# A fused attention and FFN layer on one core: the head of the program reordered, row norms on ScalarE, and new tables of the order

## The reference

```python
xn = _layernorm(x, axis=-1)                          # (x - m) / sqrt(v + eps)
# attention: 16 heads of 8 channels, scale 1/sqrt(8), causal
Q = _rope(split_heads(xn @ wq.T), 10000.0)
K = _rope(split_heads(xn @ wk.T), 10000.0)
V = split_heads(xn @ wv.T)
scores = jnp.einsum('bhqd,bhkd->bhqk', Q, K) * scale
scores = jnp.where(causal_mask, -jnp.inf, scores)
out = jnp.einsum('bhqk,bhkd->bhqd', jax.nn.softmax(scores), V)
attn = merge_heads(out) @ wo.T
ffn = jnp.einsum('bsk,nk->bsn', xn, CB) * (SCB * (1.0 / 127.0)) + bias
return x + attn + ffn
```

## Time and profile before

| | us |
|---|---|
| median of 3 runs | 260.01 |
| lowest and highest | 258.69 and 260.51 |
| the profiled execution | 259.88 |
| its span | 258.2 |
| TensorE busy | 240.1 (93%) |
| VectorE busy | 218.7 (85%) |
| ScalarE busy | 183.6 (71%) |
| GpSimd busy | 103.6 (40%) |

### The profile page before, as it was taken

The page is one execution under the profiler, slowest core; times in us unless marked ns, Lnnn a source line. Parts: engine busy times, 40 slices in busy tenths (PEclk is TensorE's granted clock), DMA queues, the critical chain, the costliest instruction groups (busy, mean ns, idle before and its releaser), DMA issues.

```text
span 258.2 us, 10150 instructions
## 1 busy us (share of the span) xinstructions
PE 240.1 (93%) x4294; PEld 124.1 (48%) x4294; DVE 218.7 (85%) x594; ACT 183.6 (71%) x360; POOL 103.6 (40%) x169
## 2 busy tenths in 40 slices
PE   6888896888999999999999999999999999999945
PEld 6546541233344555554554465445555554436334
DVE  7899268999999999989999998999889989962072
ACT  2045732273997888779788878889889799999701
POOL 7570724749856391293233032304401430440300
PEclk9999998699999999999999999999999999999997
DMA  7625758620230467162027103700770210010602
GB/s 196 220 66 150 202 120 156 144 46 4 67 85 23 106 165 129 44 165 67 5 81 165 29 4 103 158 18 3 192 163 5 90 41 4 3 44 20 182 10 84
DMA packets 23559, 22.96 MB, mean 89 GB/s; under 512 B 2757, under 2 KB 20549, under 8 KB 23513
## 3 DMA queue, kind: packets, MB, share of 16 engines
q1 hardware_dynamic: 23368, 22.05, 34.3%
q10 hardware_dynamic: 144, 0.26, 0.4%
HBM read 13.70 MB, written 8.39 MB: 86 GB/s over the span
## 4 chain that ended last, share of the span: by engine, by line
PE 72%; DVE 13%; ACT 5%; DMA 4%; SPq 2%; issue 2%; POOL 1%; ACTq 0%
PE psA L918 22%; PE psB L918 20%; PE psV L990 18%; DVE prod L802 8%; ACT ring L697 3%; PE psB L906 2%; PE psB L901 2%; PE psA L1030 2%; DMA qs<-shiftsT 2%; SPq L384 2%; DMA rest<-o_scratch 2%; PE psA L872 1%; DVE rest L815 1%; PE psB L872 1%; ACT xnT L639 1%
## 5 line engine op out<-in xcount | busy, mean ns | idle before, releaser
L802 DVE CUSTOM_DVE_ANT_0 prod<-psA,cmask 128x128 f32<-128x128 f32 (+7 forms) x256 | 177.9, 754 | 16.7 <-PE psA L918 15.6
L697 ACT ACTIVATE ring<-psB 128x512 f32<-128x512 f32 x288 | 154.5, 608 | 33.6 <-PE psB L918 30.7
L918 PE MATMUL psB<-qs,ks 128*32 128x512 bf16 (+3 forms) x1536 | 99.2, 327 | 0.5 <-DMA qs<-shiftsT 0.2
L918 PE MATMUL psA<-ks,qs 128*32 128x512 bf16 (+3 forms) x1536 | 94.7, 334 | 5.3 <-DVE mx L802 4.5
L990 PE MATMUL psV<-ring,va 128*32 128x512 f32 (+3 forms) x768 | 76.0, 486 | 0.1
L918 PEld LDWEIGHTS psB<-qs,ks 128*32 128x32 bf16 x1536 | 40.8, 96 | 48.6 <-ACT ring L697 24.2
L559 POOL TENSOR_SCALAR_AFFINE_SELECT ring<-ring 128x512 f32<-128x512 f32 x64 | 40.0, 642 | 48.2 <-ACT ring L697 48.2
L918 PEld LDWEIGHTS psA<-ks,qs 128*32 128x32 bf16 x1536 | 34.2, 96 | 43.8 <-DVE mx L802 28.0
L539 POOL CAST shifts<-mx 128x16 bf16<-128x16 f32 x16 | 3.2, 198 | 71.0 <-DVE mx L802 71.0
L990 PEld LDWEIGHTS psV<-ring,va 128*32 128x32 f32 x768 | 22.5, 110 | 16.6 <-issue 8.9
L802 DVE DVE_READ_ACCUMULATOR2_ANT mx<- 128x1 f32 x256 | 21.3, 83 | 0.0
(11 more groups left out here) (89 smaller groups left out, 157.0 us busy)
## 6 DMA issues: line engine op xcount, KB each, us to landing
qs<-q_scratch SPq DMA_DIRECT2D x48, 96.0 KB
ks<-k_scratch SPq DMA_DIRECT2D x48, 96.0 KB
o_scratch<-ot SPq DMA_DIRECT2D x12, 256.0 KB, 2.6
q_scratch<-ot SPq DMA_DIRECT2D x20, 128.0 KB, 2.5
k_scratch<-ot SPq DMA_DIRECT2D x12, 128.0 KB, 2.5
x_sb<-x SPq DMA_DIRECT2D x4, 256.0 KB, 4.5
rope_sb<-rope SPq DMA_DIRECT2D x2, 512.0 KB, 6.8
rot<-o_scratch SPq DMA_DIRECT2D x3, 256.0 KB, 3.5
```

The costliest lines, as they stand in the source:

```text
L697: act.activation(ring[:, s % P_RING, k * HALF:(k + 1) * HALF], bank_b(e % B_RING), ACT.Exp)\
L802: last = dve.tensor_tensor_reduce(masked_scores[:, u % 2, at:at + w], psA[:, (u % 2) * SEQ + at:(u % 2) * SEQ + at + w], cmask[:, SEQ - w: ...
L918: mm = pe.matmul(psum[strip:strip + STRIP, at:at + size], keys[:, strip:strip + STRIP], queries, start=True, stop=True)
```

## The change

1. The third part of chunk 3 moves from GpSimd to VectorE, and the one of chunk 1 on VectorE stands ahead of rows 2 and 3's norms, which VectorE no longer does. ScalarE normalises rows 2 and 3: Identity with scale rstd and bias mean_shift = -mean x rstd, two new small steps of GpSimd per row (scales, mean_shifts). Row 3's statistics stand on VectorE behind chunk 3's third part.
2. Four tasks, not five, stand ahead of the first unit. The transposes of row 3 and their wait for four saved tasks stand behind unit 0 (TURN_AFTER), task v1 and the others behind later units.
3. ScalarE's queue stores the third part of chunk 1 and loads the three key stacks of quad 0's first half; SyncE no longer does. SyncE stores quad 0's shifts ahead of the loads of quads 1 and 2.
4. Chunk 5 is kept in ot, not in xn, so the save of quad 1's half 0 waits for its third part.
5. All tables are new.

```diff
-TASKS = [("v", 0), ("ffn", 0), ("late", 4), ("late", 5), ("v", 1), ("ffn", 1), ("late", 6), ("late", 7),
-         ("max", 0)]
-FIRST_TASKS = 5
+TASKS = [("v", 0), ("ffn", 0), ("late", 4), ("late", 5), ("v", 1), ("ffn", 1), ("max", 0), ("late", 6), ("late", 7)]
+FIRST_TASKS = 4
-TASK_AFTER = {(5, 0): 0, (5, 1): 1, (6, 0): 2, (6, 1): 2, (7, 0): 3, (7, 1): 3, (8, 0): 8}
+TURN_AFTER = 0
+TASK_AFTER = {(4, 0): 2, (4, 1): 4, (5, 0): 5, (5, 1): 7, (6, 0): 10, (7, 0): 11, (7, 1): 13, (8, 0): 15, (8, 1): 18}
...
 VALUE_BANK = [
-    [7, 8, 13, 27, 29, 31, 33, 39, 44, 45],
+    [7, 9, 13, 28, 30, 32, 35, 40, 45, 50],
...
-    [11, 20, 22, 26, 29, 32, 35, 37, 37, 38],
+    [12, 15, 17, 21, 24, 27, 30, 35, 35, 36],
...
 SAVE_BANK = [
...
-    [23, 43],
+    [18, 40],
...
-LATE_SPLIT = [[-2, -2, 11], [-2, 10, 23], [8, 17, 35], [11, 22, 45]]
+LATE_SPLIT = [[-2, 9, 15], [-2, 19, 25], [-2, 21, 25], [19, 40, 59]]
-LATE_BANK = [[1, 4], [7, 28], [26, 30], [28, 49]]
+LATE_BANK = [[7, 9], [8, 30], [29, 31], [33, 52]]
...
-PROJECT_BANK = [269, 276, 296]
-TURN_FIRST = 292
+PROJECT_BANK = [261, 271, 290]
+TURN_FIRST = 285
...
+            def mean_shifts(g):
+                bt = slice(4 * g, 4 * g + 4)
+                pool.wait_ge(rstd_ready, g + 1)
+                pool.tensor_tensor(mean_shift[:, bt], mv[:, bt, 0], rstd[:, bt], ALU.mult).then_inc(shift_step, 1)
+                pool.wait_ge(shift_step, g - 1)
+                pool.tensor_scalar(mean_shift[:, bt], mean_shift[:, bt], -1.0, None, ALU.mult).then_inc(shift_ready, 1)
...
+            def normalise(g):
+                act.wait_ge(shift_ready, g - 1)
+                for t in range(4 * g, 4 * g + 4):
+                    act.activation(xn[:, t, :], x_sb[:, t, :], ACT.Identity, bias=mean_shift[:, t:t + 1],
+                                   scale=rstd[:, t:t + 1]).then_inc(xn_late_ready, 1)
...
             turned_rows(2)
+            act.wait_ge(part3[1], 1)
+            act.dma_start(scratch[1][:, 2, :, 0:HALF], part(1, 2)).then_inc(scratch_out[0], 16)
             save_task(0)
-            turned_rows(3)
             parts_of(2, 0)
+            act.wait_ge(pads0_ready, 2)
+            act.wait_ge(scratch_out[0], 16 * ROUND_DMAS)
+            for g in range(PARTS):
+                act.dma_start(ks[g * GROUP:(g + 1) * GROUP, 0, 0, :, :],
+                              scratch[1][0:QUAD, 0:PARTS, :, 0:HALF].rearrange("h p d t -> (p d) h t"))\
+                    .then_inc(stack_in[0][0], 16)
             save_task(1)
             parts_of(3, 0)
             parts_of(2, 1)
             parts_of(3, 1)
+            save_task(2)
+            save_task(3)
+            normalise(3)
+            turned_rows(3)
...
                         scores(i, u)
+                        if i == 0 and u == TURN_AFTER:
+                            pe.wait_ge(task_saved, FIRST_TASKS)
+                            turn_rows(3)
```

More of the change, by code:

```diff
@@ L421, in _ @@
             load_stack(0, 1)
+            store_shifts(0, 0)
             sp.wait_ge(pads1_ready, 2)
@@ L424, in _ @@
             load_stack(1, 1)
-            store_shifts(0, 0)
+            store_shifts(0, 1)
             sp.wait_ge(pads2_ready, 2)
@@ L428, in _ @@
             load_stack(2, 1)
-            store_shifts(0, 1)
             for i in range(1, QUADS):
@@ L481, in _, with scales @@
             pads(qs, 1, 0.0, pads1_ready)
-            for g in range(4):
+            def scales(g):
                 bt = slice(4 * g, 4 * g + 4)
@@ L680, in _ @@
             parts_of(3, 1)
-            for n in range(2, len(TASKS)):
+            save_task(2)
+            save_task(3)
+            normalise(3)
+            turned_rows(3)
+            for n in range(FIRST_TASKS, len(TASKS)):
                 save_task(n)
@@ L703, in save @@
                 act.wait_ge(pv_done, i * NSTEPS + LAST[i][hf] + 1)
+                if i == 1 and hf == 0:
+                    act.wait_ge(part3[5], 1)
                 act.activation(ot[:, i, hf * HALF:(hf + 1) * HALF], psV[:, :], ACT.Copy).then_inc(ot_saved, 1)
@@ L759, in _ @@
             statistics(2)
-            statistics(3)
             def leave(c):
@@ L781, in rotate, with third_part @@
                                   ALU.add).then_inc(rotated, 1)
+            def third_part(c):
+                dve.wait_ge(part2, c + 1)
+                dve.tensor_tensor(part(c, 2), rest[:, c % 2, :], part(c, 1), ALU.subtract).then_inc(part3[c], 1)
             rotate(0)
@@ L794, in _ @@
             leave(3)
+            third_part(3)
+            statistics(3)
             def maximum(i, u):
@@ L864, in turn_rows @@
                 for t in range(4 * g, 4 * g + 4):
-                    pe.wait_ge(xn_ready, t + 1)
+                    if g < 2:
+                        pe.wait_ge(xn_ready, t + 1)
+                    else:
+                        pe.wait_ge(xn_late_ready, t - 7)
                     mm = pe.transpose(turn_bank(g)[:, (t % 4) * P:(t % 4 + 1) * P], xn[:, t, :], ident[:, :])
@@ L889, in task @@
                 if m == 0:
-                    pe.wait_ge(xnT_ready, 4 if n else 2)
+                    pe.wait_ge(xnT_ready, 2 if n == 0 else 3 if n < FIRST_TASKS else 4)
                     if n >= 2:
```

70 lines of the change are left out of this document (40 added, 30 removed), and 26 rows, old and new, of tables (UNIT_BANK, VALUE_BANK).

## The result

The changed kernel took 262.93 us (median of 4 executions, 262.37 to 264.25), the kernel before in the same comparison 259.62 (258.69 to 260.51): ratio 1.0124, 95% interval 1.0079 to 1.0170. The profiled execution took 262.37 us with a span of 260.6, against 259.88 and 258.2.

The account below looks back on a forecast made before the run. VectorE was taken to set the pace to about 80 us, TensorE behind that. Span 258.2 + 2.8 (bank 72, net of the 1.8 head start) - 2.0 (end) = 259.0, hence 260.7 us; range 255.8 to 263.7.

Parts of the forecast that it names:

- the forecast's own 258.6 to 262.4: Whole program: time if bank 72 waits and the start gains 0.5 to 3 us; chance 0.5.
- rival 2: Start: half clock slows the half tasks by 3.0 us, 1.8 ahead becomes 1.2 behind, 263.7 us; chance 0.2 with rival 3.
- the prediction's own signs of being wrong: No TensorE wait over 1 us at bank 72, a second such gap at another bank, or unit 4 later than 39.
- Start of quad 0: Quad 0's maxima end at 56.1 instead of 57.90, 1.8 us ahead; upper bound 3.0.
- The chain to row 3's norms: Start: ScalarE's last part, VectorE's third part and statistics, GpSimd's steps, then four norms put unit 1 at 33.9 us.
- Unit 0 near 27.5: Start: with less ahead in TensorE's queue, unit 0 can be scored near 27.5 us instead of 31.08.
- quad 0's end to be passed on one to one: Between quad 0 and bank 10: quad 0's end sets TensorE's progress there in both kernels, so the 1.8 us carries on.
- The wait at bank 72: Quad 1: chunk 7's later third part delays the shift, TensorE waits some 4.7 us, bank 72 starts 2.8 later than before.
- the lower bound's reason: Bank 72: if the shift landed in 2.85 us, as at 59.77, the wait is 3.1 us.
- the third: Rival 3, start: unit 1 later than 35 us for want of statistics, 262 to 263 us; chance 0.2 with rival 2.
- The end: Quad 7: saving half 0 at bank 18 instead of 23 brings psV's copy 2.35 us sooner; net 2.0 (1.2 to 2.4).
- Other tables 0: Other table entries move work between banks where TensorE is busy anyway: 0 us (-1 to +1).

Follow-up runs that it names:

- f1: e1 plus dummy transposes on TensorE, 8 ahead of unit 0 and 24 behind it: 256.26 us, ratio 0.9866 to the kernel before.
- e1: Changed kernel with chunk 7's third part back ahead of GpSimd's FFN additions, ScalarE's part 2 at bank 49: 256.6 us, ratio 0.9869 to the kernel before.
- e2: Changed kernel with quad 0's last values behind bank 45 instead of 50: 256.73 to 261.8 us, ratio 0.9882 to the kernel before.
- e4: Changed kernel with row 3's transposes behind unit 2 of quad 0 instead of unit 0: 263.02 us, ratio 1.0113 to the kernel before.
- g1: Kernel before with the change's tables of quads 5 to 7, PROJECT_BANK and TURN_FIRST: 259.14 to 264.96 us, ratio 1.0006.
- g3: e1 with earlier row 3 statistics, dummy transposes, row 3's transposes behind unit 1, chunk 1's store and key loads on SyncE: 253.83 to 259.67 us, ratio 0.9837.
- g4: The changed kernel again without edit, in a later comparison: 258.67 to 264.9 us in ten executions, ratio 1.0003 to the kernel before.
- f4: e1 with the store of chunk 1's third part and three key loads back on SyncE's queue: 254.86 to 260.75 us, ratio 0.9867.
- e3: Kernel before with the change's tables of quad 7 alone, PROJECT_BANK and TURN_FIRST: 258.7 us, ratio 0.9934.

## Why the prediction was right in its range and off in its terms

The forecast was 260.7 (span 259.0), +2.8 at bank 72 and -2.0 at the end. Measured in the span: +4.1 at quad 2, +1.7 behind, -3.4 at the end. The measured 262.93 us lies inside the stated range, but just outside the forecast's own 258.6 to 262.4: only the room left for the rivals holds it. The start came out as rival 2 had it, 1.1 us behind where that rival said 1.2, and one of the prediction's own signs of being wrong occurred: unit 4 came later than 39 us (39.36).

**Start of quad 0: the step that failed.** "1.8 us ahead" was 1.1 behind. The chain to row 3's norms was right in kind (last part 27.6 for 27.9, mean_shift ready at 31.75 for 31.85), its norms cost 1.65 where I had 1.1, and unit 1 came at 34.99 for 33.9. I had interpolated the norm from copies without an operand for scale or bias. The Trainium skill, ScalarE: Activation LUTs, section What ACT_TABLE_LOAD costs, gives 186 ns plus 0.833 a column and 93 ns for each pointer operand, an estimate of 479 ns for this one; the trace has 483 ns as the mean of the eight. Against the forecast of 56.1 the miss at quad 0's end was 2.9 us. The norms are 0.55 of it. The second rival is 1.8 (after against f1; 0.9 in an execution in which the clock fell early), where I had priced it at 3.0. The last 0.5 is the half tasks between the later units, which I had charged 0.5 for: with the clock up, unit 4 to the end still took 19.4 us in f1 against 18.4 before. Keeping the clock up alone, I would have got 57.2 at quad 0's end, not 56.1. "Unit 0 near 27.5" failed too: TensorE's queue was free at 27.8 and the keys came 1.30 us later, at 29.10, a wait that I had put at nothing. It cost nothing here, because unit 1 stood behind row 3's norms.

**From there to bank 10 and 36.** I took quad 0's end to be passed on one to one. TensorE began bank 10 1.0 us later, as that says, but at quad 1 only 0.27 was left. From the exponential of bank 10 to that of bank 36 every traced kernel with the changed tables took 16.7 us and every one with the old ones 17.5: the tables gain 0.8 us there, which I had put at nothing.

**The wait at bank 72: right.** The mechanism, its two entries and its chain on GpSimd's and SyncE's queues happened as written; e1 and e2 take it away, whole and in part. The size: TensorE idled 3.4 us within 103.5 to 108 for 4.7, mainly because bank 72 began 3.35 us after the shift's issue, not 4.39, which was the lower bound's reason. In time it cost 3.7 us. (The prediction's sign for the store of keys, 94 to 95 us, didn't fit its own 96.1 for the third part; it went out at 96.70.) What I had not seen is that such a wait is followed by a fall of the clock in most executions traced (after, e2, e4, g1, g3, with waits of 2.0 to 2.9 us; not g4 with 2.8, nor f4 with 1.7), 1.4 to 1.7 us more in the kernels with the changed tables.

**The end: right in sign, too small, and by another mechanism.** I had 2.0 us for the earlier copy of psV at the head of the chain. The copy came 2.4 us sooner against quad 7's first exponential, as forecast (10.7 us behind it for 13.1), but it left the chain altogether, with the round trip, and the end took 2.8 to 3.4 us less (2.8 in e3, 2.9 in e1). "Other tables 0" held from quad 2 to 7 once the rows are whole: 119.5 against 119.3 us.

That the sum came out near is luck in part: the misses of +1.3 (start and wait) and +1.7 (clock) were set against -1.4 (end), and nothing in the working links them. The chances of rival 2 (0.2 with the third) were too low for something that the trace of before already showed.
